# Second merge of a two-layer edge convolution: slope and addition of x from PSUM by half superblocks, statistics by pairs of blocks

## The reference

```
def _egnn_conv(x, src, dst, edge_attr, W_msg, W_edge, W_root, b):
    msg = x[src] @ W_msg + edge_attr @ W_edge
    agg = jax.ops.segment_max(msg, dst, num_segments=x.shape[0])
    agg = jnp.where(jnp.isneginf(agg), 0.0, agg)
    return agg + x @ W_root + b
c1 = leaky_relu(_egnn_conv(X, ..., W1_...))          # slope 0.01
c2 = leaky_relu(_egnn_conv(c1, ..., W2_...))
out = _layernorm(x + c2, axis=-1)                    # mean and variance over 96 values, eps 1e-5, no weights
```

## Time and profile before

| | |
|---|---|
| median of 3 runs | 1866.52 us |
| the profiled execution's own time | 1874.13 us |
| its span | 1872.3 us |
| VectorE busy | 1315.3 us (70%) |
| ScalarE busy | 1080.9 us (58%) |
| TensorE busy | 1525.2 us (81%) |
| GpSimd busy | 1089.0 us (58%) |
| mean granted clock of TensorE | 0.948 |

### The profile page before, as it was taken

One profiled execution on the slowest core, in us unless ns is written; L12 is line 12 of the kernel. 1 busy time (PEld: TensorE's weight loads), 2 busy tenths in 40 slices (PEclk: granted clock), 3 DMA queues, 4 the chain that ended last, 5 costly groups with the idle time before them and its releaser, 6 DMA issues.

```text
span 1872.3 us, 37110 instructions
## 1 busy us (share of the span) xinstructions
PE 1525.2 (81%) x11422; PEld 1355.2 (72%) x11422; DVE 1315.3 (70%) x2385; ACT 1080.9 (58%) x2450; POOL 1089.0 (58%) x1454
## 2 busy tenths in 40 slices
PE   3998888888889999896889899988987767676663
PEld 2677777777779888885777777777777666576653
DVE  2677677667766655554667777767636789999998
ACT  2354544444543555563555555555527788888887
POOL 6777777767710000004777777777657788675653
PEclk9999999999999999998999999999989899988887
DMA  7778998889875788895878888888767899999996
GB/s 137 212 206 259 285 268 263 263 254 261 261 248 163 239 264 275 284 290 170 223 224 228 238 223 235 233 226 241 205 222 214 248 288 305 296 297 295 294 300 174
DMA packets 505022, 459.13 MB, mean 245 GB/s; under 512 B 348553, under 2 KB 412340, under 8 KB 504836
## 3 DMA queue, kind: packets, MB, share of 16 engines
q1 hardware_dynamic: 444118, 321.15, 60.0%
q0 software_dynamic: 30976, 57.72, 12.3%
q10 hardware_dynamic: 29742, 77.88, 10.6%
HBM read 283.25 MB, written 173.37 MB: 244 GB/s over the span
## 4 chain that ended last, share of the span: by engine, by line
PE 30%; DVE 24%; DMA 20%; POOL 15%; issue 9%; ACT 1%; SPq 1%; DVEq 0%; POOLq 0%; ACTq 0%
PE ps L584 19%; DMA onehot_bytes<-arena_hold 14%; POOL arena_hold L410 12%; DVE stats L953 5%; DMA arena_hold<-nodes,src_perm 4%; DVE arena_hold L896 4%; DVE arena_hold L951 4%; PE ps L495 4%; DVE arena_hold L948 4%; POOL onehot L443 3%; PE ps L463 2%; PE ps L486 2%; DVE arena_hold L882 2%; PE ps L456 2%; DVE arena_hold L971 1%
## 5 line engine op out<-in xcount | busy, mean ns | idle before, releaser
L584 PE MATMUL ps<-arena_hold,onehot 128*128 x4688 | 614.4, 293 | 174.7 <-POOL onehot L443 142.7
L584 PEld LDWEIGHTS ps<-arena_hold,onehot 128*128 128x128 f32 x4688 | 584.1, 206 | 205.3 <-issue 204.2
L410 POOL DMA_INDIRECT arena_hold<-nodes,src_perm x392 | 370.0, 944 | 459.9 <-SPq L377 340.7
L495 PEld LDWEIGHTS ps<-w_root,onehot 97*128 97x128 f32 x3136 | 402.4, 194 | 100.9 <-issue 99.0
L410 POOL DMA_INDIRECT arena_hold<-in_x_dram,src_all x392 | 375.1, 957 | 143.7 <-issue 115.2
L495 PE MATMUL ps<-w_root,onehot 97*128 97x128 f32 x3136 | 418.9, 277 | 0.0
L443 POOL CAST onehot<-keep 128x256 f32<-128x256 uint8 x588 | 302.3, 562 | 117.4 <-PE ps L584 71.6
L648 ACT COPY arena_hold<-ps 128x384 f32<-128x384 f32 x392 | 187.9, 479 | 277.3 <-PE ps L495 275.0
L698 ACT COPY arena_hold<-ps 128x384 f32<-128x384 f32 x392 | 166.7, 477 | 200.3 <-PE ps L584 200.2
L882 DVE TENSOR_TENSOR_SCAN arena_hold<-keep,arena_hold,ps 96x512 f32<-96x512 bf16 x196 | 247.6, 1263 | 42.1 <-PE ps L463 41.8
L896 DVE TENSOR_TENSOR onehot<-count,rel 128x1024 f32<-128x1024 bf16 x147 | 179.5, 1222 | 126.9 <-PE ps L584 126.0
(11 more groups left out here) (99 smaller groups left out, 1160.9 us busy)
## 6 DMA issues: line engine op xcount, KB each, us to landing
root<-arena_hold ACTq DMA_DIRECT2D x196, 384.0 KB
arena_hold<-root SPq DMA_DIRECT2D x196, 384.0 KB, 4.6
nodes<-arena_hold SPq DMA_DIRECT2D x98, 384.0 KB, 3.0
arena_hold<-nodes SPq DMA_DIRECT2D x98, 384.0 KB
arena_hold<-in_x_dram SPq DMA_DIRECT2D x97, 384.0 KB
arena_hold<-in_x_dram SPq DMA_DIRECT2D x48, 768.0 KB, 8.1
out_dram<-arena_hold SPq DMA_DIRECT2D x48, 768.0 KB, 4.7
onehot_bytes<-arena_hold SPq DMA_DIRECT2D x147, 128.0 KB
```

Source lines behind the costliest of these rows:

```text
L410: nc.gpsimd.indirect_dma_start(out=gathered[t.ring][0:t.p, i, 0:D], out_offset=None, in_=table_in, in_offset=bass.IndirectOffsetOnAxis(ap= ...
L495: last = nc.tensor.matmul(no_ps[m % 2][:, i * P:(i + 1) * P], nodes_t[m % NODE_RING][0:D + 1, i * P:(i + 1) * P], w_root[0:D + 1, layer * ...
L584: nc.tensor.matmul(ps_bytes[:, bass.ds(place_at, SLOT)].bitcast(F32), onehot[:, k % NS, i, :], rows_from(t)[:, bass.ds(word, SLOT)].bitcas ...
```

## The change

VectorE now works by halves. `slope_and_add(h)` replaces the first part of `finish(s)`: ScalarE's evacuation of the second layer no longer copies but writes 0.01 times the bank to `nodes_out`; VectorE takes the maximum of that (SBUF) and the bank (PSUM) and writes it back into the bank; it then adds x (SBUF) to the bank (PSUM) and writes the sum to `nodes_out`. `bn_stats` runs over two blocks at once, through an access pattern that takes an element of the one block and an element of the other in turn, so that its "even" and "odd" results are the two blocks' own mean and spread; there are 8 in place of 16, and lines 961 to 964 go. ScalarE's square root takes the spread directly, with scale 1/96. ScalarE normalises 12 blocks (14 in superblocks 46 and 47, 7 in the last), VectorE four (2, 7). A bank of PSUM may be seeded again only when x has been added. ScalarE's order becomes, in half h: (h even) `deviation(s - 1)`, evacuate, reseed for half h - 1, normalise blocks 0 to 6; (h odd) evacuate, normalise blocks 7 to 11, reseed for half h - 1. So halves are reseeded one half later than before. `load_x(s)` waits for the same point of the work, counted in halves. The first merge does the same as before in its own function.

```diff
-        stats = sb("stats", [P, RI, 6], F32)
-        small = sb("small", [P, 9, RI], F32)
+        stats = sb("stats", [P, RI // 2, 6], F32)
+        small = sb("small", [P, 5, RI], F32)
...
-            return LAST_BLOCKS // 2 if s == NSB - 1 else 15 if s >= NSB - 3 else 13
+            return LAST_BLOCKS // 2 if s == NSB - 1 else 14 if s >= NSB - 3 else 12
...
+        dev, inv, shift = small[:, 0, :], [small[:, 1 + i, :] for i in range(2)], [small[:, 3 + i, :] for i in range(2)]
+        both = stats[:].rearrange("p j (h c) -> p j h c", c=3)
+        mean, spread = both[:, :, :, 1], both[:, :, :, 2]
...
-                    sp.wait_ge(vec_2, X_ADDED * (s - 2) + X_ADD)
+                    sp.wait_ge(x_added, 2 * (s - 1))
...
-                    act.wait_ge(evacuated[layer], n - RING + 1)
+                    if layer == 0:
+                        act.wait_ge(evacuated[0], n - RING + 1)
+                    else:
+                        act.wait_ge(x_added, (n - RING) // HG + 1)
...
+            def evacuate(layer, h):
+                s = h // 2
+                for n in range(h * HG, (h + 1) * HG):
+                    at = n % SG * C * D
+                    to, of = nodes_out[s % 3][:, at:at + C * D].rearrange("p (j d) -> p j d", d=D), slot[:, n % RING, :, 0:D]
+                    if layer == 0:
+                        nc.scalar.copy(to, of).then_inc(evacuated[0], 1)
+                    else:
+                        nc.scalar.activation(to, of, ACT.Copy, scale=SLOPE).then_inc(evacuated[1], 1)
...
+            def merge_out():
+                first_seeds(1)
+                for h in range(2 * NSB):
+                    s = h // 2
+                    if h % ENDS == 0:
+                        ends = load_ends(h)
+                    if h % 2 == 0 and s:
+                        deviation(s - 1)
+                    if h % 2 == 0 and s >= 3:
+                        act.wait_ge(out_stored[s % 3], DMA * (s // 3))
+                    act.wait_ge(stepped[1], ends[h % ENDS])
+                    evacuate(1, h)
+                    if h % 2 == 0:
+                        if s:
+                            reseed(1, h - 1)
+                            normalise(s - 1, 0, ACT_FIRST)
+                    else:
+                        if s:
+                            normalise(s - 1, ACT_FIRST, scalar_blocks(s - 1))
+                        reseed(1, h - 1)
+                deviation(NSB - 1)
+                normalise(NSB - 1, 0, scalar_blocks(NSB - 1))
...
-                nc.scalar.activation(small[:, 3, :], small[:, 2, :], ACT.Sqrt, bias=eps[:, 0:1]).then_inc(dev_done, 1)
+                nc.scalar.activation(dev.rearrange("p (j h) -> p j h", h=2), spread, ACT.Sqrt, bias=eps[:, 0:1], scale=1.0 / D).then_inc(dev_done, 1)
...
+            def slope_and_add(h):
+                s, blocks = h // 2, min(HG * C, LAST_BLOCKS - HG * C) if h == 2 * NSB - 1 else HG * C
+                at = h % 2 * HG * C * D
+                y, x_rows = (a[s % 2 if a is x_in else s % 3][:, at:at + blocks * D] for a in (nodes_out, x_in))
+                done = slot[:, h * HG % RING:h * HG % RING + HG, :, 0:D]
+                y_all = nodes_out[s % 3][:, at:at + HG * C * D]
+                dve.wait_ge(evacuated[1], (h + 1) * HG)
+                nc.vector.tensor_tensor(done, done, y_all.rearrange("p (b j d) -> p b j d", b=HG, d=D), ALU.max).then_inc(sloped, 1)
+                if h % 2 == 0:
+                    tail = 1 if s == NSB - 1 and N_END % P else 0
+                    dve.wait_ge(x_back[s % 2], DMA * (s // 2 + 1 + tail))
+                dve.wait_ge(sloped, h + 1)
...
+                    nc.vector.tensor_tensor(y.rearrange("p (b j d) -> p b j d", b=HG, d=D), done, x_rows.rearrange("p (b j d) -> p b j d", b=HG, d=D),
+                                            ALU.add).then_inc(x_added, 1)
...
+                dve.wait_ge(x_added, h + 1)
+                for j in range(0, blocks, 2):
+                    last = nc.vector.bn_stats(stats[:, h % 2 * HG * C // 2 + j // 2, :], y[:, j * D:(j + 2) * D].rearrange("p (h d) -> p d h", h=2))
+                if h % 2:
+                    last.then_inc(var_done, 1)
...
-                next_step(nc.vector.scalar_tensor_tensor(y, y, SLOPE, y, ALU.mult, ALU.max))
...
-                next_step(nc.vector.tensor_tensor(y, y, x_in[s % 2][:, 0:blocks * D], ALU.add))
-                for j in range(blocks):
-                    last = nc.vector.bn_stats(stats[:, j, :], y[:, j * D:(j + 1) * D])
-                next_step(last)
...
-                nc.vector.tensor_tensor(diff, even, odd, ALU.subtract)
-                next_step(nc.vector.tensor_reduce(both, stats[:].rearrange("p j (h c) -> p j c h", c=3)[:, :, 1:3, :], mybir.AxisListType.X, ALU.add))
-                then(nc.vector.scalar_tensor_tensor(diff, diff, 0.25, diff, ALU.mult, ALU.mult))
-                nc.vector.scalar_tensor_tensor(var, spread, 1.0 / D, diff, ALU.mult, ALU.add).then_inc(var_done, 1)
...
             for s in range(NSB):
-                finish(s)
+                slope_and_add(2 * s)
+                slope_and_add(2 * s + 1)
+                normalise_own(s)
```

More of the change, by code:

```diff
@@ L32 @@
 LAG = 2
+ACT_FIRST = 7
 UNIT_RING = 4
@@ L685, in seed, with first_seeds @@
                                ).then_inc(seeded[layer], 1)
-            def merge(layer):
+            def first_seeds(layer):
                 for n in range(RING):
@@ L701, in reseed @@
[L701 to L713, removed]
-                        deviation(s - 1)
-                    reseed(2 * s + 1)
-                    if layer == 1 and s:
-                        normalise(s - 1)
@@ L718, in merge, with reseed @@
-                if layer == 1:
-                    deviation(NSB - 1)
-                    normalise(NSB - 1)
+            def reseed(layer, h):
+                for n in range(h * HG + RING, min((h + 1) * HG + RING, NG)):
+                    seed(layer, n)
+            def evacuate(layer, h):
[7 more added lines that the diff above has]
+                        nc.scalar.activation(to, of, ACT.Copy, scale=SLOPE).then_inc(evacuated[1], 1)
@@ new lines, in merge_nodes @@
+            def merge_nodes():
+                first_seeds(0)
+                for h in range(2 * NSB):
+                    s = h // 2
+                    if h % ENDS == 0:
+                        ends = load_ends(h)
+                    if h % 2 == 0 and s >= 3:
+                        act.wait_ge(nodes_stored[s % 3], 2 * DMA * (s // 3))
+                    act.wait_ge(stepped[0], ends[h % ENDS])
+                    evacuate(0, h)
+                    reseed(0, h)
+            def merge_out():
+                first_seeds(1)
+                for h in range(2 * NSB):
+                    s = h // 2
+                    if h % ENDS == 0:
+                        ends = load_ends(h)
+                    if h % 2 == 0 and s:
+                        deviation(s - 1)
+                    if h % 2 == 0 and s >= 3:
+                        act.wait_ge(out_stored[s % 3], DMA * (s // 3))
[11 more added lines that the diff above has]
+                normalise(NSB - 1, 0, scalar_blocks(NSB - 1))
@@ new lines, in slope_and_add @@
+            def slope_and_add(h):
[10 more added lines that the diff above has]
+                dve.wait_ge(sloped, h + 1)
+                parts = [(b, min(C, blocks - b * C)) for b in range(-(-blocks // C))]
+                if blocks == HG * C:
+                    nc.vector.tensor_tensor(y.rearrange("p (b j d) -> p b j d", b=HG, d=D), done, x_rows.rearrange("p (b j d) -> p b j d", b=HG, d=D),
+                                            ALU.add).then_inc(x_added, 1)
+                else:
+                    for b, n in parts:
+                        part = slice(b * C * D, (b * C + n) * D)
+                        last = nc.vector.tensor_tensor(y[:, part].rearrange("p (j d) -> p j d", d=D), done[:, b, 0:n, :],
+                                                       x_rows[:, part].rearrange("p (j d) -> p j d", d=D), ALU.add)
+                    last.then_inc(x_added, 1)
+                dve.wait_ge(x_added, h + 1)
[3 more added lines that the diff above has]
+                    last.then_inc(var_done, 1)
@@ L970, in finish @@
                     own = y[:, j * D:(j + 1) * D]
-                    last = nc.vector.tensor_scalar(own, own, inv[:, j:j + 1], shift[:, j:j + 1], ALU.mult, ALU.add)
+                    last = nc.vector.tensor_scalar(own, own, inv[s % 2][:, j:j + 1], shift[s % 2][:, j:j + 1], ALU.mult, ALU.add)
                 last.then_inc(norm_v, 1)
```

45 lines of the change are left out of this document (15 added, 30 removed).

## The result

| | before | after |
|---|---|---|
| median, us (8 runs each) | 1870.81 | 1854.39 |
| ratio, with its 95% interval | | 0.9918 (0.9894 to 0.9942) |
| span of the profiled execution, us | 1872.3 | 1851.7 |
| root of superblock 1, last root, us | 1423.7, 1864.6 | 1404.0, 1843.9 |
| us from root to root, mean of 47 | 9.38 | 9.36 |

"Root" is `deviation`, once a superblock. With eight runs the median before is 1870.81 us. The forecast was 1815 us; the measured 1854 us lies in the stated range, but the gain of 16 us is about a third of the 51 us forecast. In the two traces almost all of it lies at the start, where superblock 1 is done 20 us earlier. Of these, 3.3 us come from stages that the change does not touch: the first cast of the second merge is at 1369.2 us before and at 1365.9 after. The other 16.3 us are the change's.

The account below looks back on a forecast made before the run. VectorE was taken to bound the later stretch, at 9.13 us a superblock. Start 1409 + 47 x 8.6 + end 7.7 = 1820.9 us span, against 1872.3; the difference taken off the median gave 1815 us, range 1798 to 1872.

Parts of the forecast that it names:

- Prices of the operations: VectorE's work per superblock: slope and addition +0.15 us, statistics -0.45, small operations -1.07, one more own block +0.3.
- The alternating read: In the statistics, bn_stats reading two blocks 384 bytes apart in turn was taken to run at full rate, saving 0.45 us.
- VectorE's chain of 8.4 us: Second merge: VectorE's work and waits from one square root to the next were to take 8.4 us a superblock.
- The failed step: Second merge: seeds come a half later, but TensorE still has two seeded halves, some 28 steps, ahead; no cost was added.
- The output's store: SP's queue: issued at 2.0 us, 5.0 us to land, needed 0.22 us after the next root, so it needs 6.8 us.
- The x load: SP's queue: needs a period of 7.7 us, or 8.7 with a root load ahead, said to lie just under the period.
- Early stretch: From 1413 to 1512 us: nine superblocks fall from 11.0 to 8.6 us each, 22 us; TensorE's wait for GpSimd nearly gone.
- held-up casts: Rival: operations with a PSUM and an SBUF operand still delay GpSimd's casts; 24 us lost early, 1839 us, chance 0.06.
- The DMA bound: Rival: the DMA engines become the bound at 298 GB/s, period 9.0 us, 1834 us, chance 0.17.
- The half-priced read: Rival: the statistics' alternating read costs half of line 844's excess, +1.07 us, period 9.4 us, 1853 us, chance 0.14.
- the slower rival: The statistics' alternating read costs line 844's whole excess or more; at 1.47 ns an element +2.26 us, 1904 us, chance 0.10.
- the second pass: Rival: writing a PSUM bank in place takes a second pass, +1.6 us, period 10.0 us, 1881 us, chance 0.06.

Follow-up runs that it names:

- experiment 9: The changed kernel with SP's queue reordered (root unit, store, x load, root unit) and GpSimd waiting for seeds batch by batch: 1812.11 us, 0.9688 of the kernel before.
- experiment 12: The changed kernel with SP's queue reordered, GpSimd opening single batches, and one of 16 x blocks loaded from the third superblock on: 0.9677 of the kernel before.
- SP's order: The changed kernel with SP's round reordered to root unit, store of the output, load of x, root unit: 0.9855 of the kernel before.
- experiment 2: The changed kernel with only one of the 16 blocks of x loaded per superblock from the third on: 0.9862 of the kernel before.
- experiment 4: The kernel before the change with only one of the 16 blocks of x loaded per superblock from the third on: 0.9997 of the kernel before.
- The statistics alone: The kernel before with only bn_stats over pairs of blocks and no small operations, slope and addition still in SBUF: 0.9942 of the kernel before.
- the PSUM part alone: The changed kernel with one bn_stats a block and the four small operations back, slope and addition still from PSUM: 1.0075 of the kernel before.
- the best version: The changed kernel with both SP's queue reordered and GpSimd opening batches singly: 1812.11 us, 0.9688 of the kernel before.

## Why the prediction was wrong

- **Prices of the operations: right.** Slope and addition, the statistics, the small operations, the end (7.8 us, 7.7 forecast), the casts. The alternating read, the dispute of the forecast, costs nothing. The Trainium skill's Vector Engine (DVE) Microarchitecture Reference, section 5.2, had the two cases, and its exception (one stream alternating between two regions) is the one that the trace bears out, at 0.27 us from start to start.
- **VectorE's chain of 8.4 us: right, but hidden.** It shows in 8.36 us periods of several of the kernels, and in experiment 9 as the mean of 8.42. The forecast gave 8.6 us for it with DMA: 1409 + 47 x 8.6 + 7.7. The kernel after is 1404.0 + 47 x 9.36 + 7.8 = 1851.7. So the start was 5 us better than forecast, 3.3 us of them because the merge began earlier in this execution, and 47 x 0.76 = 36 us are the error. Against the chain alone, 8.4 us, the loss is 47 x 0.96 = 45 us; the 0.2 us that the forecast added were for the DMA engines, which experiment 12 shows not to bind.
- **The failed step** is the sentence "Seeds come a half later; TensorE still has two seeded halves, some 28 steps, ahead". The forecast put the later seeds at no cost. It looked at TensorE's steps and not at the queue that feeds them. GpSimd waits for `seeded` too, at a coarser grain: a pair of 16 steps, and a late superblock has about 20 steps, so two seeded halves are about 20 steps there and not 28. The signs were there: the kernel before waits at line 437 for the seeds of a whole pair of batches, and its trace had GpSimd waiting 40.4 us for them (1420 to 1850 us), which the forecast did not price. Opening by single batches, which leaves the seeds as they are and changes only that grain, gives 0.9807 for 0.9918, and VectorE's wait for evacuations falls from 25.7 to 10.0 us. That shows it. The output's store is not the cause: with SP's order ScalarE has no wait for it, and 22.1 us of VectorE's wait are left. How much of it TensorE's lower clock adds stays open.
- **The x load: the mechanism was named, its size taken as nothing.** "These loops lie just under the new period" stood beside a bound of 8.7 us, against a chain of 8.4. The bound itself was too low: 384 KB at the 304 GB/s of the earlier trace rows are 1.3 us and not 1, and the landing became 9.0 us (8.2 before). The bound was not put into the sum either. VectorE waits 16.3 us for x and ScalarE 8.1 us for the store. SP's order gives 0.0063 alone, and 0.0119 (0.9807 to 0.9688) once the seeds are in time.
- **Early stretch.** "TensorE's wait for GpSimd nearly gone" was wrong: 25.3 us before, 21.5 after. The held-up casts are gone, the seeds' wait took their place: GpSimd waits 17.4 us for seeds from 1413 to 1512 us, 1.6 before. In experiment 9 15.0 us are left, with a clock of 0.97 (0.86 before) and periods of 8.4 to 8.5 us from the fourth on.
- **The rivals.** The DMA bound is refuted by experiments 2, 4 and 12. The half-priced read gave 1853 us, which the result met by chance; its mechanism is refuted. (Its period of 9.4 us is also 0.1 to 0.2 us too long by the forecast's own working: 8.4 + 1.07, less the 0.2 us that the slower rival takes off, is 9.3, or 1847 us.) Neither the second pass nor the held-up casts exist.
- **Where the gain lies.** The statistics alone give 0.9942, the PSUM part alone 1.0075, both 0.9918. By themselves they would add to 1.0017. The PSUM part lengthens VectorE's work and frees the casts; the statistics shorten it and, alone, leave the casts held up. Only with both is VectorE's chain so short that the seeds and SP's queue hold it up by 42 us.

Not tried: a third buffer for x, which would test the load's lead in another way; and a run that keeps TensorE's clock up and leaves the seeds late, which would part the two.

## What to carry to other kernels

When a buffer is given back later, list every engine that waits for its refill, with the grain at which it waits, and not only the engine that works in it. When a step moves past a square root or any other point of meeting, walk each in-order queue once with the new times: a load issued one wait later here lost most of a period of lead. And take two waits away together before judging either, as one may hide part of the other.

## What the runs showed of the hardware

- `bn_stats` over two blocks read in turn, 384 bytes apart, runs at the full rate (duration ns min/median/max; a single block has a mean of 243 ns), 105 ns more for 96 columns more:

```profile
L992 DVE BATCH_NORM_STATS2 stats<-arena_hold x391: 336/348/370, 1385.5 to 1843.5; 128x6 f32<-128x192 f32 x196
```

- The slope (line 975) reads and writes the same banks of PSUM: 959 ns in the mean, against 958 for the addition that writes to SBUF.
- TensorE's granted clock fell from 1.00 to 0.50 while it stood idle for 3.51 us in the chain of waits above; 23 of its records then took 4.96 us, and 41 took 4.79 us at 1.00.
- A DMA share of 1.0 was no ceiling. The kernel before had 1.02 at 304 GB/s, the best version 1.08 at 330 GB/s, with the same transfers in the merge.
- Sixteen times fewer and longer pieces for the x load (6144 in place of 384 bytes) shortened its landing only from 9.0 to 8.3 us.
